# Token rows of the expert tiles transposed by DMA, and the third weight matrix fetched from DRAM by tile

## The reference

```python
        gate = xf @ Wg.T + bg
        vals, idx = jax.lax.top_k(gate, TOP_K)          # TOP_K = 1
        probs = jax.nn.softmax(vals, axis=-1)
        dispatch = jnp.sum(jax.nn.one_hot(idx, E, dtype=x.dtype) * probs[..., None], axis=1)
        h = jax.nn.silu(jnp.einsum('td,efd->tef', xf, W1)) * jnp.einsum('td,efd->tef', xf, W2)
        out = jnp.einsum('tef,edf,te->td', h, W3, dispatch)
```

## Time and profile before

| | |
|---|---|
| median of 3 runs | 896.97 us (894.79 to 901.04) |
| span of the profiled execution | 896.9 us |
| PE busy | 808.7 us, 90% of the span |
| DVE busy | 724.7 us, 81% |
| ACT busy | 610.4 us, 68% |
| POOL busy | 279.6 us, 31% |
| expert stage, first gather issued to last scatter issued | 741.1 to 888.9 us |

### The profile page before, as it was taken

How to read it: one execution, slowest core, us unless ns; L and a number is a source line. 1 busy time by engine, 2 the same in 40 slices (tenths; PEclk the granted TensorE clock), 3 DMA queues, 4 the chain that set the end, 5 groups by cost and what they waited for, 6 DMA issues and landing times. The chain is left out here.

```text
span 896.9 us, 26204 instructions
## 1 busy us (share of the span) xinstructions
PE 808.7 (90%) x8970; PEld 447.6 (50%) x8970; DVE 724.7 (81%) x1022; ACT 610.4 (68%) x1139; POOL 279.6 (31%) x437
## 2 busy tenths in 40 slices
PE   4999749999999999999999999999988617999994
PEld 1668713333333333333333333333368517999994
DVE  5966777998889989989998999989437585888883
ACT  3776616888888888888888888888845603454442
POOL 6620000022343423202232233421115304566552
PEclk9999958999999999999999999999999657999997
DMA  6356963444545445344444444543044502222310
GB/s 173 88 146 209 352 207 86 112 131 124 137 131 135 136 120 133 110 120 123 133 128 131 135 136 137 147 124 95 3 164 131 175 0 74 78 82 82 93 56 11
DMA packets 69734, 109.63 MB, mean 122 GB/s; under 512 B 20140, under 2 KB 36682, under 8 KB 68147
## 3 DMA queue, kind: packets, MB, share of 16 engines
q1 hardware_dynamic: 59120, 75.49, 29.6%
q0 software_dynamic: 9248, 26.51, 10.3%
q10 hardware_dynamic: 1314, 6.95, 2.0%
HBM read 77.58 MB, written 33.19 MB: 124 GB/s over the span
## 5 line engine op out<-in xcount | busy, mean ns | idle before, releaser
L906 DVE TENSOR_REDUCE neg_max<-max_ps 128x1 f16<-128x1024 f32 x384 | 452.3, 1222 | 52.6 <-PE max_ps L760 52.2
L889 ACT ACTIVATE probs<-ring_ps 128x512 f32<-128x512 f32 x768 | 413.6, 595 | 69.3 <-PE ring_ps L792 67.7
L792 PE MATMUL ring_ps<-q_side,k_side 113*128 113x512 f16 x768 | 234.6, 387 | 5.6 <-DMA q_side<-rel_split 3.6
L804 PE MATMUL out_ps<-probs,values 128*32 128x256 f32 x3072 | 206.4, 386 | 0.1
L760 PE MATMUL max_ps<-k_side,q_side 48*128 48x256 f16 x1536 | 122.8, 279 | 14.5 <-DMA q_side<-rel_split 8.3
L804 PEld LDWEIGHTS out_ps<-probs,values 128*32 128x32 f32 x3072 | 80.3, 109 | 111.0 <-ACT probs L889 56.5
L656 POOL COPY max_copies<-neg_max 128x32 f16<-128x32 f16 x48 | 10.1, 210 | 365.6 <-DVE neg_max L906 365.6
L760 PEld LDWEIGHTS max_ps<-k_side,q_side 48*128 48x128 f16 x1536 | 50.0, 95 | 113.8 <-issue 65.5
L792 PEld LDWEIGHTS ring_ps<-q_side,k_side 113*128 113x128 f16 x768 | 51.8, 97 | 104.3 <-ACT probs L889 72.9
L1460 PE MATMUL hid_ps<-slot_t,w_top 128*118 128x128 f16 x312 | 69.7, 223 | 0.8 <-ACT slot_t L1506 0.8
L1461 PE MATMUL hid_ps<-slot_t,w_top 128*118 128x128 f16 x312 | 69.0, 221 | 0.0
(11 more groups left out here) (230 smaller groups left out, 1322.2 us busy)
## 6 DMA issues: line engine op xcount, KB each, us to landing
q_side<-rel_split SPq DMA_DIRECT2D x384, 64.0 KB, 2.2
q_side<-qk_split SPq DMA_DIRECT2D x192, 64.0 KB, 2.4
rel_split<-expert_weights ACTq DMA_DIRECT2D x6, 1024.0 KB, 5.1
rel_split<-expert_weights SPq DMA_DIRECT2D x6, 1024.0 KB, 6.1
q_side<-qk_split SPq DMA_DIRECT2D x48, 128.0 KB, 2.7
k_side<-qk_split SPq DMA_DIRECT2D x144, 32.0 KB, 1.8
token_rows<-tn_parts SPq DMA_DIRECT2D x8, 512.0 KB, 3.4
expert_weights<-in_w_t POOLq DMA_DIRECT2D x32, 117.2 KB, 2.9
```

Source lines behind the costliest of these rows:

```text
L792: nc.tensor.matmul(ring_ps[turn_of(k) % BANKS][:], k_side[slot(s)][:, tile * P:(tile + 1) * P], q_side[slot(s)][:, tile // 2, (i % 2) * HA ...
L804: last = nc.tensor.matmul(out_ps[quarter * 2 * HD:(quarter + 1) * 2 * HD, :], values[j][:, tile, :], probs[:, u % 2 * GROUP + 2 * i + quar ...
L889: nc.scalar.activation(probs[:, u % 2 * GROUP + i, :], ring_ps[turn_of(k) % BANKS][:], ACT.Exp).then_inc(exp_done, 1)
L906: nc.vector.tensor_reduce(neg_max[:, j % 2, t:t + 1], max_ps[t % 2][:], AX, ALU.max, negate=True).then_inc(tile_max, 1)
```

## The change

Three things are altered.

First, PE no longer transposes the token rows and ACT no longer copies them from PSUM. SP, which had no part in `experts`, issues one transposing DMA for each tile (`dma_start_transpose`, from the gathered rows to `slot_t`, 128 x 512 float16 or 128 KB), two tiles ahead.

Second, W3 of each tile is no longer copied by DVE from a store in SBUF. SP loads the tile's expert index into a register (`value_load`) and issues a transfer of 384 KB from DRAM (`w3_split`) straight into the tile's buffer, also two tiles ahead. Third, the store in SBUF (`g.w3`) and the four transfers that filled it in `gate` are gone.

```diff
@@ gate @@
-            load_experts(sp, g, experts_loaded)
...
-            sp.wait_ge(experts_loaded, 16 * (EXPERTS // 2))
...
@@ experts @@
-        t_ps = psum("slot_ps", [P, 2 * HALF], F16)
...
+        @block.sync
+        def _(sp):
+            by_row = g.w3_split.rearrange("e k f -> k e f")
+
+            def load_output(n, j):
+                e = sp.value_load(g.tile_expert[0:1, bass.ds(n, 1)], min_val=0, max_val=EXPERTS - 1)
+                sp.dma_start(w3[:, j:j + 1].rearrange("k s q c d -> k s (q c d)"), by_row[:, bass.ds(e, 1)]).then_inc(w3_loaded[j], 16)
+
+            def turn_rows(j, loads):
+
+                sp.wait_ge(rows_loaded[j], 16 * loads)
+                sp.dma_start_transpose(tt[:, j % S], parts_of(j)).then_inc(t_loaded[j % S], 16)
+
+            sp.wait_ge(g.w3_stored, 16 * EXPERTS)
+            for n in range(S - 1):
+                load_output(n, n)
+            for n in range(S - 1):
+                turn_rows(n, 1)
+
+            def step(s):
+                if s.before(1) and s.after(S - 1):
+
+                    sp.wait_ge(h_ready, 2 * s.n)
+                if s.after(S - 1):
+                    turn_rows((s.slot + S - 1) % R, s.group + (s.slot + S - 1) // R + 1)
+                if s.before(1):
+
+                    sp.wait_ge(y_ready, s.n)
+                if s.after(S - 1):
+                    load_output(s.n + S - 1, (s.slot + S - 1) % S)
+
+            for n in range(N_T):
+                step(Step(n, n // R, n % R, N_T, True))
...
         @block.tensor
         def _(pe):
-            def transposes(n, group, j, reused):
...
-            def output(n, j, reused):
+            def output(n, j, loads, reused):
                 pe.wait_ge(hid_lo_done, n + 1)
-                pe.wait_ge(w3_taken, n + 1)
+                pe.wait_ge(w3_loaded[j], 16 * loads)
...
-                pe.wait_ge(t_copied, s.n + 1)
+                pe.wait_ge(t_loaded[j], 16 * ((R // S) * s.group + s.slot // S + 1))
...
                 hidden(j, 0)
-                if s.after(1):
-                    transposes(s.n + 1, s.group + (s.slot + 1) // R, (s.slot + 1) % R, True)
                 hidden(j, 1)
...
         @block.scalar
-                if s.after(1):
-                    copy_t(s.n + 1, (j + 1) % S, s.before(2))
...
         @block.vector
-                if s.after(2) and s.before(1):
-
-                    take_output(e, two)
```

More of the change, by code:

```diff
@@ L984, in gate @@
         g_ps = psum("gate_ps", [P, TT * 2 * EXPERTS])
-        experts_loaded, ones_set, rows_zeroed, warmed = sem("experts_loaded"), sem("gate_ones"), sem("rows_zeroed"), sem("warmed")
+        ones_set, rows_zeroed, warmed = sem("gate_ones"), sem("rows_zeroed"), sem("warmed")
         at_ps_ready, at_ready, proj_ready, x1_ready = sem("at_ps_ready"), sem("at_ready"), sem("proj_ready"), sem("x1_ready")
@@ L1227, in _ @@
             nc.vector.tensor_tensor(g.gates[:], by_part[:, :, 1, :], g.gates[:], ALU.add).then_inc(gate_copied, 1)
[L1230 to L1235, removed]
 def inverse_root(nc, dve, stats, mean, var, rstd, shift, tmp, eps, chain, root, root_done, shift_done, tiles=slice(0, TT), calls=0):
@@ L1401, in experts @@
         psum = lambda name, shape, dt=F32: ctx.enter_context(nc.psum_tensor(name, shape, dt))
-        t_ps = psum("slot_ps", [P, 2 * HALF], F16)
         h_ps = [[psum(f"hid{h}_ps{i}", [FC, HALF]) for h in range(2)] for i in range(S)]
         y_ps = psum("y_ps", [P, HALF])
-        top_taken, tail_taken, w3_taken = sem("top_taken"), sem("tail_taken"), sem("w3_taken")
+        top_taken, tail_taken, w3_loaded = sem("top_taken"), sem("tail_taken"), [sem(f"expert_w3_loaded{j}") for j in range(S)]
         rows_loaded = [sem(f"rows_loaded{j}") for j in range(R)]
-        t_ready, t_copied = sem("slot_t_ready"), sem("slot_t_copied")
+        t_loaded = [sem(f"slot_t_loaded{j}") for j in range(S)]
         h_ready, silu_done, hid_done = sem("h_ready"), sem("silu_done"), sem("hid_done")
@@ L1477, in output @@
                 last.then_inc(y_ready, 1)
-            transposes(0, 0, 0, False)
             def step(s):
@@ L1489, in step @@
                 hidden(j, 0)
-                if s.after(1):
-                    transposes(s.n + 1, s.group + (s.slot + 1) // R, (s.slot + 1) % R, True)
                 hidden(j, 1)
                 if s.before(1):
-                    output(s.n - 1, (j - 1) % S, s.before(2))
+                    output(s.n - 1, (j - 1) % S, (R // S) * s.group + (s.slot - 1) // S + 1, s.before(2))
             steps(pe, N_T, R, step)
-            output(N_T - 1, (N_T - 1) % S, True)
+            output(N_T - 1, (N_T - 1) % S, (N_T - 1) // S + 1, True)
         @block.scalar
         def _(act):
[L1501 to L1508, removed]
             def step(s):
@@ L1541, in take_hidden @@
                 nc.vector.tensor_copy(w_tail[:, j:j + 1].rearrange("p s h f -> p s (h f)"), tails[:, bass.ds(e, 1), :]).then_inc(tail_taken, 1)
-            def take_output(e, j):
-                nc.vector.tensor_copy(w3[:, j:j + 1].rearrange("k s q c d -> k s (q c d)"), g.w3[:, bass.ds(e, 1)]).then_inc(w3_taken, 1)
             expert_of = lambda n: dve.value_load(g.tile_expert[0:1, bass.ds(n, 1)], min_val=0, max_val=EXPERTS - 1)
[L1547 to L1551, removed]
+            for n in range(2):
+                take_hidden(expert_of(n), n)
             def step(s):
@@ L1675, in build @@
         g.slot_rows = sb("slot_rows", [P, R, ROW])
-        g.w3 = sb("w3_all", [P, EXPERTS, 2 * W3], F16)
         gate(nc, g)
```

## The result

The changed kernel took 902.26 us (median of 15 runs, 897.06 to 908.69) against 897.25 us before; the ratio is 1.0053, 95% interval 1.0028 to 1.0077. It is slower by about 5 us, where 6.4 us less was forecast. The profiled execution has a span of 902.1 us. Two executions lie more than 1.5% above the fastest of their kernel, one of nine of e4 (1518 us) and one of ten of e6 (912 us), and are left out of the ratios.

The account below looks back on a forecast made before the run. PE was taken to bound the expert stage; -8.4 us for transposes leaving PE, +1.3 and +0.7 us at the start, sum -6.4 us, giving 890.6 us from the median 896.97. Range 886.5 to 918 us.

Parts of the forecast that it names:

- The bound and the prize: Expert stage: PE sets the pace; removing four transposes saves 0.22 us a tile; relief of ACT and DVE is worth nothing.
- the sum's -8.4 us: Flow of the expert stage: 38 sets of transposes leave PE at 0.22 us each.
- The start: Up to the first hidden matmul: +1.3 us for the DMA transpose, +0.7 us for two W3 loads beside the first gather.
- Test 2: DMA engines per tile: 1.05 + 1.0 + 0.5 = 2.55 us against PE's 3.28, share near 0.78; fits, with queueing.
- test 3: SP's chain from W3 load to transposed tile: 5.2 us, transpose 2.7, within two steps of 6.56 us; 1.4 us to spare.
- its sign of being wrong: A transpose's issue to landing, forecast 2.7 us; above 4.5 us the prediction counts itself wrong.
- B: SP's single stream makes transposed tiles late, PE waits at L1473; 899 to 918 us, middle +11; chance 0.20.
- C: DMA engines full as the transpose breaks into small pieces: 4.55 us a tile, +40, 939 us; chance 0.12.
- D: Transposes go block by block and set the pace: 7.2 us a tile, +147, 1044 us; chance 0.08.
- The gate stage: Four W3 load issues by SP leave it; costed at nothing, at most 1 us gain.

Follow-up runs that it names:

- e4: Against the kernel before: DMA transposes only from tile 3, the first three tiles by PE and ACT, W3 still copied by DVE; 893.33 us, ratio 0.9930.
- e6: Changed kernel with nine buffers for token rows and results instead of six, so gathers run eight tiles ahead, not five; ratio to before 1.0030.
- e11: The kernel before, unchanged, timed and profiled once more; ratio to itself 1.0002.
- e1: Kernel before with only the transposes moved to DMA from SP; W3 stays in its SBUF store, copied by DVE; 893.24 us, ratio 0.9952.
- e2: Kernel before with only W3 loaded from DRAM by SP for each tile; PE and ACT transpose as before; ratio 1.0023.
- e5: Changed kernel with the first two transposes placed ahead of the first two W3 loads in SP's order; ratio to before 1.0021.
- e9: Kernel e4 plus a 384 KB load per tile, issued by ACT into a spare buffer nobody reads; ratio to before 1.0025.
- e7: Changed kernel with index loads and W3 loads issued by ACT, only the transposes on SP; ratio to before 1.0089.
- e3: Changed kernel with the first three tiles transposed by PE and copied by ACT, DMA transposes from tile 3; 899.25 us, ratio to before 1.0021.
- e8: Changed kernel fetching only the high half of W3 (192 KB) from tile 3 on; one run, 38 steps in 127.8 us.
- e12: Kernel e4, unchanged, timed once more; ratio to before 0.9936.

## Why the prediction was wrong

**The bound and the prize: right.** PE sets the pace, four transposes cost 0.22 us a tile, and nothing on ACT or DVE mattered. A step without them is 3.23 us (forecast 3.28), 0.22 us less than the commonest step of e11, 3.45, and e4's stage is 8.7 us shorter, for a forecast of 8.4 us. The gain was there and was given back twice: of the sum's -8.4 us for the flow 2.4 were left, and the start took 6.5 instead of 2.0. Together that is +4.1 us, where the stage has +3.9.

**The start: the first step that failed, 4.5 us.** It was costed at +1.3 for the transpose and +0.7 for W3's loads, +2.0 in all, and came to +6.5 us. Of the parts alone the transpose's was sized right (e1 has +1.3 us with no W3 traffic), W3's too low (e2 has +1.9 us with W3 alone, the upper end of the 0 to 1.9 given). Together they are +6.5, 3.3 us more than the sum of the two, because the late gathers and the first transposes then meet: the transpose took 6.1 us, not 2.7. e5 undoes it by order alone. The error was to take the transpose's latency from rows of other stages, without a term for what stands before it in the queue, and to take the two costs as independent.

**Test 2, the DMA engines: the second step that failed, with test 3 worth 6.0 us in the flow.** The forecast was 2.55 us a tile. Measured: gathers and scatters 1.16 instead of 1.05 (0.360 x 3.22), W3 1.31 instead of 1.0, transposes 0.72 instead of 0.5, together 3.2 us for a step of 3.23. These prices are shares of packet time and move with what runs beside them: the gathers and scatters alone filled 29.5% of the engines before, 24.2% in e2, 36.0% in e1 and 39.5% in the changed kernel, for 6.8 to 7.4 MB in 80 us. "It fits, with queueing" was the sentence to stop at: a share of 0.78 was already a warning, and my sum had no term for waiting in the queue. I took W3 at the rate of a transfer that ran alone, and had the better figure, 1.4 us, beside it.

**Test 3, the lead: right in its shape, wrong in the transpose's 2.7 us.** SP's issue of a transpose was 1.2 us (forecast 0.5) and the W3 issue 0.35 (0.5). The transpose took 2.7 us from issue to first use in e1's start, as forecast, but 3.5 to 3.6 us to its landing at the median in the flow of e1 and e4, and 4.7 to 5.8 us in the seven late steps of the changed kernel. That is over the 4.5 us which the prediction itself named as its sign of being wrong. SP's issue stands 5.0 us before the use at the median, so the three with 5.3 to 5.8 us were late by their landing alone; the four with 4.7 to 4.9 us had also been issued late, only some 4 to 4.5 us before PE was ready for them. The test also left out a wait: the transposed tile needs the gathered rows, which POOL fetches two steps before SP wants them and which now land in 4.6 us at the median. e6 shows that this wait alone decided nothing.

**The rivals.** B, SP's chain, was priced at +11. Its sign came (PE waits at L1473, landings over 4.5 us), but not its cause: e9 has late tiles with no W3 load in SP's stream, and e7 points the same way. C, full DMA engines, is nearest to what happened, though not as described: I had it begin where the engines' work exceeds PE's step, so at +40 us. In fact the work stays just under the step, the pace remains PE's in most tiles, and seven steps are 0.4 to 1.0 us longer. The case between "fits" and "sets the pace" was missing. D, block by block, did not occur: 0.72 us for all four.

The runs bear out neither of the two statements on transposing DMAs in full. The Trainium skill's "TRN2 transpose DMAs are as fast as regular DMAs" ("Advanced Engine Details and Errata", X-Bar Transpose (TRN2)) agrees with e1's start (2.7 us, as for a plain 128 KB in the earlier trace rows), while as load 131 KB cost 0.72 us, 182 GB/s, less than half of the 410 GB/s of the plain load in the earlier trace rows. The Trainium skill's 1309 ns a block ("VectorE: DVE Perf Modes", The three transpose paths), times four, was not seen as a price of each tile: with no W3 traffic the median from issue to landing is 3.5 us for four blocks.

**The gate stage** was costed at nothing. The loads taken out of it show nowhere: up to the first gather it took 80.1 to 81.8 us in six profiles without them (e2, e3, e5 to e8) and 80.6 and 81.8 in the two of before, 85 in the changed kernel and in the five of the other kernels that keep them.

## What to carry to other kernels

Two transfers that each hide need not hide together: add up the load of all queues for one step of the loop, take each price from rows with traffic beside it, and treat a high share as a case of its own, with single late tiles: here at shares of 0.59 to 0.63 at most one step of 38 was late, at 0.76 and above four to thirteen. Of a change in two halves, weigh each: here one half (transposes off PE) was worth 8 us of the stage and 6 us of the time, and the other (W3 from DRAM) had no gain to offer, since the copy that it removed lay beside the bound, and it used up the engines that the first half needed. Where a pipeline is filled, the old path may serve for the first tiles: PE's transposes for three of 39 tiles (e4, e12) kept the start at 5.3 us, and that kernel beats both, at 893 us, 0.993 and 0.994 of before.

## What was not expected of the hardware

- A transposing DMA of 128 x 512 float16 from SBUF to SBUF moves in some 548 packets of under 512 bytes, takes 1.2 us of SP to issue and 0.72 us of all 16 engines. From issue to use it took 2.7 us at e1's start; in the flow it landed after 3.5 us at the median at a share of 0.59 (e4), and after 4.1 us at 0.98 (changed).
- Reading 384 KB from DRAM tile by tile cost 1.31 us of all engines, beside gathers, where four such larger transfers alone had run at 410 GB/s, 0.96 us.
- The same gate stage took 80 to 82 us or 85 us up to the first gather, with dips of PE's granted clock in different places; one program timed against itself spread over 894.6 to 903.4 us, with a mean granted clock of 0.950 in the shortest execution and 0.942 in the longest.
